# Attention of a four-block transformer kernel: q and k projected and split once, copied into row strips through DRAM, and scores of two heads issued together

## The reference, cut to what matters

```python
# per batch: 16 heads of width 8, sequence 256
q = split_heads(xn @ Wq.T)
k = split_heads(xn @ Wk.T)
v = split_heads(xn @ Wv.T)
s = einsum('bhqd,bhkd->bhqk', q, k) / sqrt(8) + relative_bias   # causal
y = softmax(s, -1) @ v
x = x + y @ Wo.T
```

## Time and profile before

| | |
|---|---|
| median of three executions | 2702.1 us |
| the profiled execution | 2699.89 us |
| its span, first to last instruction | 2698.1 us |
| PE busy | 2506.0 us (93%), of which fillers 491.8 us |
| DVE busy | 1943.5 us (72%) |
| ACT busy | 1612.1 us (60%) |
| POOL busy | 1367.7 us (51%) |
| mean granted TensorE clock | 0.969 |

### The profile page before, as it was taken

One profiled execution on the slowest core, in us unless ns is written; L12 is line 12 of the kernel. 1 busy time (PEld: TensorE's weight loads), 2 busy tenths in 40 slices (PEclk: granted clock), 3 DMA queues, 4 the chain that ended last, 5 costly groups with the idle time before them and its releaser, 6 DMA issues.

```text
span 2698.1 us, 41593 instructions
## 1 busy us (share of the span) xinstructions
PE 2506.0 (93%) x14781; PEld 1756.5 (65%) x14781; DVE 1943.5 (72%) x3913; ACT 1612.1 (60%) x3465; POOL 1367.7 (51%) x1227
## 2 busy tenths in 40 slices
PE   7999999997898999887899999998999999999988
PEld 7888885785565655655555765756556656566665
DVE  5878798789787788687787688788787868532420
ACT  1424436443886567653776558664976786466754
POOL 1466474847373656456363745557373738321111
PEclk9999999998998999998999999998999999999989
DMA  4123121312121113112120212122120213000000
GB/s 153 52 75 102 46 90 48 94 56 71 42 85 32 56 47 96 45 58 63 47 80 33 78 41 63 48 67 63 40 87 29 79 41 94 17 5 1 1 5 5
DMA packets 88573, 150.59 MB, mean 56 GB/s; under 512 B 10565, under 2 KB 21485, under 8 KB 88110
## 3 DMA queue, kind: packets, MB, share of 16 engines
q1 hardware_dynamic: 88366, 147.94, 17.8%
HBM read 145.26 MB, written 2.65 MB: 55 GB/s over the span
## 4 chain that ended last, share of the span: by engine, by line
PE 75%; ACT 10%; DVE 8%; issue 4%; POOL 3%; DMA 0%; POOLq 0%; SPq 0%; DVEq 0%; ACTq 0%
PE c_bank L1369 16%; PE c_bank L924 15%; PE c_bank L916 14%; PE a_bank L762 7%; PE a_bank L752 3%; PE b_bank L1083 2%; DVE hst L710 2%; PE b_bank L1072 2%; PE a_bank L731 2%; PE b_bank L584 2%; ACT weighted_y L959 1%; DVE a_bank L704 1%; PE b_bank L565 1%; PE a_bank L768 1%; PE a_bank L736 1%
## 5 line engine op out<-in xcount | busy, mean ns | idle before, releaser
L833 POOL TENSOR_TENSOR prod_c<-hst,prod_c 128x512 f32<-128x512 f32 x512 | 666.3, 1307 | 411.1 <-DVE hst L710 384.0
L710 DVE TENSOR_TENSOR_SCAN hst<-dA,a_bank 128x512 f32<-128x512 f32 x512 | 621.8, 1214 | 14.8 <-ACT dA L822 4.5
L822 ACT ACTIVATE dA<-delta,a_neg 128x510 f32<-128x510 f32 x512 | 364.7, 719 | 320.5 <-DVE hst L710 314.8
L916 PE MATMUL c_bank<-c_xT,w 128*128 128x512 f32 x1024 | 532.4, 624 | 23.5 <-ACT weighted_y L959 11.8
L924 PEld LDWEIGHTS c_bank<-w,hid 128*128 128x128 f32 x4096 | 487.5, 192 | 57.9 <-ACT hid L951 26.8
L1369 PEld LDWEIGHTS c_bank<-ident 128*128 128x128 f32 x4004 | 484.6, 193 | 47.8 <-issue 39.3
L924 PE MATMUL c_bank<-w,hid 128*128 128x128 f32 x4096 | 511.1, 277 | 1.6 <-ACT hid L951 1.5
L1369 PE MATMUL c_bank<-ident 128*128 128x128 f32 x4004 | 491.8, 277 | 0.3 <-ACT weighted_y L959 0.3
L951 ACT ACTIVATE hid<-c_bank,b 128x512 f32<-128x512 f32 x512 | 349.1, 687 | 150.0 <-PE c_bank L916 147.4
L975 POOL TENSOR_TENSOR xs<-xs,weighted_y 128x512 f32<-128x512 f32 x128 | 167.5, 1309 | 497.3 <-ACT weighted_y L959 496.2
L704 DVE TENSOR_TENSOR a_bank<-du,a_bank 128x512 f32<-128x512 f32 x512 | 349.8, 683 | 72.6 <-PE a_bank L752 69.9
(11 more groups left out here) (182 smaller groups left out, 3159.8 us busy)
## 6 DMA issues: line engine op xcount, KB each, us to landing
prod_c<-c_rows SPq DMA_DIRECT2D x512, 256.0 KB, 3.2
w<-in_w SPq DMA_DIRECT2D x2, 2048.0 KB
xs<-in_x SPq DMA_DIRECT2D x8, 256.0 KB, 7.2
bias<-skew SPq DMA_DIRECT2D x1, 2048.0 KB, 8.4
out_dram<-xs SPq DMA_DIRECT2D x8, 256.0 KB, 2.3
in_wT<-in_in_wT SPq DMA_DIRECT2D x1, 512.0 KB
c_rows<-bcC SPq DMA_DIRECT2D x16, 32.0 KB, 1.6
b_hq<-in_w_gu SPq DMA_DIRECT2D x1, 384.0 KB, 3.3
```

The source lines that it names most:

```text
L710: nc.vector.tensor_tensor_scan(hst[:, s % RS, :], dA[:, s % RA, :], b_bank, 0.0, ALU.mult, ALU.add).then_inc(M.h.sem, 1)
L822: nc.scalar.activation(half_batches(dA[:, s % RA, :], 1), half_batches(delta[:, h, :], 1), ACT.Exp, scale=a_neg[:, l, h, n:n + 1]).then_in ...
L833: nc.gpsimd.tensor_tensor(prod[:, s % RP, :], hst[:, s % RS, :], cring[:, s % RC, :], ALU.mult).then_inc(M.pp.sem, 1)
L916: nc.tensor.matmul(S.bank[up_bank(e, c)][:, :], w1[:, e, c * 128:(c + 1) * 128], S.xT[:, :], start=True, stop=True).then_inc(M.up.sem, 1)
```

## The change

In the attention block:
- wqT and wkT become plain 128x128 matrices whose rows are reordered on the host. PE makes k and q in one matmul each.
- ACT evacuates q once, scaled. DVE makes the high parts of both by masking and the low parts by subtraction: four instructions. The arrays `split`, q_all and k_all are gone.
- SP has a lane b. It writes high, high and low part of q and of k to DRAM (`qk_rows`, 128x512 each: six DMAs of 256 KB), waits for all six, and loads the result into the strips of qT and kT: eight DMAs into 24 partitions each, 192 KB each.
- Scores are issued for two heads at a time, 2w and 2w+1, whose strips are neighbours: the two matmuls with 256 keys, then the two with 128. The even head goes to bank 0, the odd one to bank 1. The next pair waits until DVE is done with both.
- The transposes of the exponentials move from bank 1 to bank 2, the first columns of which the matmuls with v also write. Those of the next four heads therefore wait for the end of the chain of the last four (M.y). `pr` has four buffers. The transposes of heads 2w-2 and 2w-1 stand behind the scores of pair w, and the matmuls with v directly behind those of their fourth head.
- All five order strings are new. Lane d has 1816 fillers in place of 2002.

```diff
-        att_buf = sb("att_buf", [128, 2 * 384 + 3 * 384])
+        att_buf = sb("att_buf", [128, 2 * 384 + 4 * 384])
         sc = att_buf[:, 0:768].rearrange("p (b n) -> p b n", b=2)
-        pr = att_buf[:, 768:1920].rearrange("p (b n) -> p b n", b=3)
-        q_hi, q_all, k_hi = (att_buf[:, i * TOK:(i + 1) * TOK] for i in range(3))
+        pr = att_buf[:, 768:2304].rearrange("p (b n) -> p b n", b=4)
+        q_hi, k_hi, k_lo = (att_buf[:, i * TOK:(i + 1) * TOK] for i in range(3))
...
-        k_all = flat(sbb.xn[:, :, :])
+        q_lo = flat(sbb.xn[:, :, :])
...
-            for g in range(HG):
-                dve.wait_ge(M.qE.sem, L.at(M.qE, g + 1))
-                nc.vector.tensor_scalar(q_hi.bitcast(I32), q_hi.bitcast(I32), TOP12, None, ALU.bitwise_and).then_inc(L.sem, L.one())
-                yield
...
-                nc.vector.tensor_scalar(k_hi.bitcast(I32), S.bank[1][:, :].bitcast(I32), TOP12, None, ALU.bitwise_and).then_inc(M.kH.sem, 1)
-                yield
-                dve.wait_ge(L.sem, here)
-                nc.vector.scalar_tensor_tensor(out=qT[:, g, :], in0=q_hi, scalar=split[:, 0:1], in1=q_all,
-                                               op0=ALU.mult, op1=ALU.add).then_inc(M.qS.sem, 1)
-                yield
-                dve.wait_ge(M.kH.sem, L.at(M.kH, g + 1))
-                nc.vector.scalar_tensor_tensor(out=kT[:, g, :], in0=k_hi, scalar=split[:, 2:3], in1=k_all,
-                                               op0=ALU.mult, op1=ALU.add).then_inc(M.kS.sem, 1)
-                yield
+            dve.wait_ge(M.qE.sem, L.at(M.qE, 1))
+            nc.vector.tensor_scalar(q_hi.bitcast(I32), q_lo.bitcast(I32), TOP12, None, ALU.bitwise_and).then_inc(M.qH.sem, 1)
+            yield
+            dve.wait_ge(M.k.sem, L.at(M.k, 1))
+            nc.vector.tensor_scalar(k_hi.bitcast(I32), S.bank[1][:, :].bitcast(I32), TOP12, None, ALU.bitwise_and).then_inc(M.kH.sem, 1)
+            yield
+            dve.wait_ge(M.qH.sem, L.at(M.qH, 1))
+            nc.vector.tensor_tensor(q_lo, q_lo, q_hi, ALU.subtract).then_inc(M.qS.sem, 1)
+            yield
+            dve.wait_ge(M.kH.sem, L.at(M.kH, 1))
+            nc.vector.tensor_tensor(k_lo, S.bank[1][:, :], k_hi, ALU.subtract).then_inc(M.kS.sem, 1)
+            yield
...
-                dve.wait_ge(M.s.sem, L.at(M.s, r + 1))
+                dve.wait_ge(M.s.sem, L.at(M.s, r // 2 + 1))
...
-                        out=sc[:, r % 2, c0:c1], in0=S.bank[0][:, c0:c1], in1=bias[:, h, b0:256], scale=1.0,
+                        out=sc[:, r % 2, c0:c1], in0=S.bank[r % 2][:, c0:c1], in1=bias[:, h, b0:256], scale=1.0,
...
-            for g in range(HG):
-                if g:
-                    pe.wait_ge(M.qE.sem, L.at(M.qE, g))
-                nc.tensor.matmul(S.bank[0][:, :], wqT[:, g, :], S.xT[:, :], start=True, stop=True).then_inc(M.q.sem, 1)
-                yield
-                if g:
-                    pe.wait_ge(M.kH.sem, L.at(M.kH, g))
-                nc.tensor.matmul(S.bank[1][:, :], wkT[:, g, :], S.xT[:, :], start=True, stop=True).then_inc(M.k.sem, 1)
-                yield
+            nc.tensor.matmul(S.bank[1][:, :], wkT[:, :], S.xT[:, :], start=True, stop=True).then_inc(M.k.sem, 1)
+            yield
+            nc.tensor.matmul(S.bank[0][:, :], wqT[:, :], S.xT[:, :], start=True, stop=True).then_inc(M.q.sem, 1)
+            yield
...
-            for r in range(NH + 4):
-                if r < NH:
-                    b, h = r // HEADS, r % HEADS
-                    g, p0, s0 = h // 4, 32 * (h % 4), b * SEQ
-                    if r == 0:
-                        pe.wait_ge(M.qS.sem, L.at(M.qS, HG))
-                        pe.wait_ge(M.kS.sem, L.at(M.kS, HG))
+            def scores(r, queries, keys, part):
+
+                b, h = r // HEADS, r % HEADS
+                p0, s0 = 32 * (h % 4), b * SEQ
+                return nc.tensor.matmul(S.bank[r % 2][:, part], qT[p0:p0 + 3 * DH, h // 4, s0 + queries:s0 + queries + 128],
+                                        kT[p0:p0 + 3 * DH, h // 4, s0:s0 + keys], start=True, stop=True)
+
+            def exp_transposes(m):
+                pe.wait_ge(M.p.sem, L.at(M.p, m + 1))
+                if m:
+                    pe.wait_ge(M.pE.sem, L.at(M.pE, m))
+                if m and m % 4 == 0:
+                    pe.wait_ge(M.y.sem, L.at(M.y, m // 4))
+                for j in range(3):
+                    ins = nc.tensor.transpose(S.bank[2][:, j * 128:(j + 1) * 128], pr[:, m % 4, j * 128:(j + 1) * 128], ident[:, :])
+                ins.then_inc(M.pT.sem, 1)
+                yield
+
+            for w in range(NH // 2 + 2):
+                if w < NH // 2:
+                    if w == 0:
+                        pe.wait_ge(s_qk, 16 * 8 * (L.g + 1))
+                        pe.wait_ge(M.kS.sem, L.at(M.kS, 1))
                         pe.wait_ge(M.vE.sem, L.at(M.vE, 1))
-                    if r:
-                        pe.wait_ge(M.m.sem, L.at(M.m, r))
-                    nc.tensor.matmul(S.bank[0][:, 0:256], qT[p0:p0 + 3 * DH, g, s0 + 128:s0 + 256],
-                                     kT[p0:p0 + 3 * DH, g, s0:s0 + 256], start=True, stop=True)
-                    nc.tensor.matmul(S.bank[0][:, 256:384], qT[p0:p0 + 3 * DH, g, s0:s0 + 128],
-                                     kT[p0:p0 + 3 * DH, g, s0:s0 + 128], start=True, stop=True).then_inc(M.s.sem, 1)
-                    yield
...
+                    if w:
+                        pe.wait_ge(M.m.sem, L.at(M.m, 2 * w))
+                    for r in (2 * w, 2 * w + 1):
+                        scores(r, 128, 256, slice(0, 256))
+                    scores(2 * w, 0, 128, slice(256, 384))
+                    scores(2 * w + 1, 0, 128, slice(256, 384)).then_inc(M.s.sem, 1)
+                    yield
+                if w >= 3 and w % 2:
+                    q = (w - 3) // 2
+                    pe.wait_ge(M.oE.sem, L.at(M.oE, q + 1))
+                    for t in range(2):
+                        ins = nc.tensor.transpose(S.bank[2][:, 256 + 128 * t:384 + 128 * t], oS[:, 128 * (1 - t):128 * (2 - t)], ident[:, :])
+                    ins.then_inc(M.oT.sem, 1)
+                    yield
+                if 1 <= w <= NH // 2:
+                    yield from exp_transposes(2 * w - 2)
+                    yield from exp_transposes(2 * w - 1)
+                if 2 <= w <= NH // 2 and w % 2 == 0:
+                    q = (w - 2) // 2
                     b = 4 * q // HEADS
                     pe.wait_ge(M.pE.sem, L.at(M.pE, 4 * q + 4))
-                    if q:
-                        pe.wait_ge(M.y.sem, L.at(M.y, q))
...
...
-                nc.scalar.activation(q_hi, S.bank[0][:, :], ACT.Copy, scale=-float(DH ** -0.5)).then_inc(L.sem, L.one())
-                yield
-                nc.scalar.activation(q_all, S.bank[0][:, :], ACT.Copy, scale=split[:, 1:2]).then_inc(M.qE.sem, 1)
-                yield
-                act.wait_ge(M.k.sem, L.at(M.k, g + 1))
-                if g:
-                    act.wait_ge(M.kS.sem, L.at(M.kS, g))
-                nc.scalar.activation(k_all, S.bank[1][:, :], ACT.Copy, scale=split[:, 3:4]).then_inc(M.kE.sem, 1)
-                yield
...
+        def b_sp(sp, L):
+
+            for g in range(GROUPS):
+                L.g = g
+                rows = a["qk_rows"][g]
+                sp.wait_ge(att.qH.sem, L.at(att.qH, 1))
+                for p in (0, 1):
+                    sp.dma_start(rows[0, p], q_hi).then_inc(s_qkd, 16)
+                sp.wait_ge(att.kH.sem, L.at(att.kH, 1))
+                for p in (0, 2):
+                    sp.dma_start(rows[1, p], k_hi).then_inc(s_qkd, 16)
+                yield
+                sp.wait_ge(att.qS.sem, L.at(att.qS, 1))
+                sp.dma_start(rows[0, 2], q_lo).then_inc(s_qkd, 16)
+                sp.wait_ge(att.kS.sem, L.at(att.kS, 1))
+                sp.dma_start(rows[1, 1], k_lo).then_inc(s_qkd, 16)
+                yield
+                sp.wait_ge(s_qkd, 16 * 6 * (g + 1))
+                for i in range(2):
+                    strips = rows[i].rearrange("p (i j g) n -> (p i) j g n", i=DH, j=4)
+                    dst = qk[:, i, :, :].bitcast(F32)
+                    for j in range(4):
+                        sp.dma_start(dst[32 * j:32 * j + 3 * DH, :, :], strips[:, j, :, :]).then_inc(s_qk, 16)
+                    yield
+
...
+    rows = [(4 * g + j) * DH + i for i in range(DH) for j in range(4) for g in range(HG)]
     for n in "qk":
...
+        out[f"w{n}T"] = A(f"L1_attn_W{n}")[rows].T
...
```

239 lines of the change are left out of this document (102 added, 137 removed).

## The result

The changed kernel takes 2610.82 us (median of four executions, 2608.57 to 2611.14). The kernel before took 2703.12 us in the same round (four executions, 2699.7 to 2706.24). The ratio to it is 0.9657, 95% interval 0.964 to 0.9674. The forecast was 2605 us. The profiled execution took 2610.92 us and its span is 2609.1, so the span fell by 89 us where the sum said 97.

A forecast was written before the change was run, and what follows sets the result against it. PE's queue was taken to set the time from 685 us on, the Mamba lane from 80 to 308. Terms summed to -97 us, a span of 2601 and a time of 2605 us; range 2535 to 2685.

The forecast's parts named there:

- Projections: PE, behind 685 us: 64 matmuls for q and k become 16, so 41 us leave PE.
- Scores: PE: with two strips side by side a pair costs what one head cost, 0.46 us, saving 59 us.
- the rival: Score pairs on PE: strips don't overlap, a pair costs 0.8 us, 47 us less relief, 2652 us; chance 0.12.
- Early fillers: PE, up to the sixth Mamba layer: 1556 become 1336, 49 us of queue, of which 30 us are gained.
- Later fillers: PE, behind the start of the sixth Mamba layer: 446 fillers become 480, adding 8 us.
- DVE and ACT: Behind 685 us: 71 us less on DVE, 60 on ACT; a tenth counts, 13 us, bounds 0 and 60.
- New waits: PE around scores: transposes share bank 2 with the matmuls with v, adding 30 us, bounds 0 and some 95.
- Strips: PE's wait for the way through DRAM ahead of first scores: 1 us for each group, 8 us.
- the slow rival: Ahead of first scores: strips arrive late, nothing lost below 1.8 us a load, 2737 us at 4; chance 0.12.
- Clock: Granted clock, a sign of being wrong if it falls: each hundredth of the mean costs PE about 27 us.
- the 180 us of waits in one rival: Whole kernel: waits left by the last plan, held against the better-plan rival, 2520 to 2580 us, chance 0.18.
- the 105 us: Gain left without the strips' term, said to be eaten by late strips from 3.7 us a load on.

The follow-up runs named there:

- one_strip: Changed kernel, but the odd head of each pair reads the even head's strip, so both matmuls stand in one row strip: 2636.96 us, ratio 0.9757.
- once: Kernel before with the changed projections, split and way through DRAM, in the old lane order, scores one head at a time: 2719.33 us, ratio 1.0061.
- The cut alone: Early fillers 1336 against 1556, all else same: kernel before with 1336 takes 2678.73 us; changed kernel with 1556 takes 2646.69, with 1336 2610.82.
- late_more: Changed kernel with 624 in place of 480 fillers behind the start of the sixth Mamba layer: 2633.38 us, ratio 0.9739.
- dve_clump: Changed kernel with twelve extra DVE copies for each group, in one piece ahead of the copy of v: 2663.85 us, ratio 0.986.

## Why the prediction was right

The time was met within 6 us, and the mechanism holds: PE's queue sets the time where attention runs, as one_strip bears out (29 us more of it cost 26), and the change made it shorter. The sum holds only in part. Ahead of the sixth Mamba layer it said -30 us and the stretch gave -12. Behind it the terms -41, -59, +8, -13, +30 and +8 make -67, and it gave -77. That one error of 18 us and one of 10 partly cancelled is luck, and not a merit of the sum. Term by term:

- **Projections, -41.** 16 records of 9.3 and 9.0 us of union, a quarter of before. Their worth alone wasn't tested: once has them, but the way through DRAM with them, and is slower.
- **Scores, -59.** Right in size on PE: a pair costs one head. Of the 59, 26 hang on the overlap (one_strip), not the 47 of the rival, which priced a pair in one strip at 0.8 us; it takes 0.60. That rival would have been 2637, not 2652.
- **Early fillers, -30.** The cut alone was worth 36, or 23 in the old kernel. But the stretch gained 12 in all, since the new order is 23 us later there, a term that the sum lacked.
- **Later fillers, +8.** At the rate of late_more, 23 for 32, they cost 5. That they hold the clock, and are worth 33 us as a whole, I hadn't seen.
- **DVE and ACT, -13.** I took a tenth of the relief, because neither engine is the limit on the whole. The prices of added DVE work, 0.38 and 0.80, would make 27 or 57 us of its 71. Neither is shown to hold for the relief, for the work removed stood in four sets and not in one piece. ACT's relief wasn't tested.
- **New waits, +30.** The idle time ahead of attention's steps from the scores on grew by 26 us, 4.5 of it for the strips: 22. With the projections' waits, which fell by 4, it is less.
- **Strips, +8.** One wait of 4.5 us. The loads were between my two ends, 1.5 us each (12.4 / 8, in one group), below the 1.8 from which the slow rival begins.
- **Clock, 0 in the sum.** It fell from 0.969 to 0.957, up to 26 us by the windows above. I had named it as a way to be wrong, with 27 us for each hundredth, and put it down to fewer fillers and shorter scores; once has neither and a clock of 0.955. Of the 52 us more at 1.2 GHz some 27 lie from 300 to 660 us, in the stretch already counted with -12. The other 25 lie behind it and cost up to 13.

If the terms simply add, the later ones as measured are -41, -59, +5, +22, +4.5 and +13, in all -55. The -77 then leave 22 us for DVE and ACT, between the 13 that I took and the 27 of the lower price. That is a remainder and no measurement: it holds whatever the new orders bring as well.

Two figures of the prediction don't come out of its rows. By the median distance between starts of each group in the trace before, the 8611 matmuls make about 2360 us, not 2518; they were used only to scale the cover of the strips and for the 180 us of waits in one rival. And by the price given for late strips, 8 x (8.5 + 8 x t - 23), the 105 us are eaten from 3.5 us on, not 3.7.

PE's busy time fell by 113.5 us, not the 130 to 140 that I gave; up to 26 us for matmuls at half clock would be the rest. For example, the experts' 4096 records of line 920 took 523.0 us, and 511.1 before. PE's idle time of 217 us lies within what I gave, and so do the first scores, 20.4 to 25.7 us behind the k projection in the eight groups (22.4 in the fourth, 1534.74 to 1557.14 on PE's timeline). No version that I ran beats the changed kernel; with 1069 early fillers it is the same.

## What to carry to other kernels

In engines with a fixed order, price work by where it stands, not by the engine's share: here DVE work added in one block ahead of another lane's chain cost 0.80 of its time, and spread in small pieces 0.38. A saving should be priced in the shape that it had, which no run here did. A detour over DRAM is free only if the order puts enough other work behind it, so plan the two together. Idle matmuls are worth keeping only up to the point where they stop covering a wait or holding the clock; count that by stretch, in both directions. And look at the clock along with the waits: in once and in dve_clump PE's idle time and the time at 1.2 GHz grew together. Which of them brought the other wasn't tested.

## What the runs showed of the hardware

- Matmuls of 24 rows in two neighbouring row strips, into two PSUM banks, start 3 ns apart and end 3 ns apart: 0.38 us for the four matmuls of a pair. The same four in one strip take 0.60, less than the 0.74 of twice a single head.
- Eight DMAs of 192 KB into 24 partitions each are issued in 3.2 us, and the last lands 9.1 us behind the end of the issues (692.21 to 701.33, one group), where a 128-partition load of 256 KB lands 3.2 us behind its own issue in the median.
- Taking filler matmuls away can lengthen a kernel: 480 fewer, 107 us of PE's time, brought the granted clock from 0.957 to 0.926 and cost 33 us.
- The clock fell without any filler or score taken away: in once, with all 2002 fillers, it is 0.955 where the kernel before has 0.969, and 0.94 in place of 0.97 in the last stretch.
